# Attention with its scores computed a second time, keys on the partitions, and its keys and values projected in the first stage

## The reference

```python
x = x + einsum('bsd,sod->bso', layernorm(x), ctx_1024[itok])   # a weight matrix picked by position, 16 of them
x = x + moe_ffn(layernorm(x))            # 8 experts, top 1, exact gelu, times the gate
def xattn(query, key, value, mask, ...): # query = layernorm(x), key = value = ctx_1024
    q, k, v = (proj(t, W, b) for ...)    # 16 heads of 16
    scores = einsum('bhqd,bhkd->bhqk', q, k) / 4 + mask * -1e9   # mask [1, 1, 256, 256]
    ctx = einsum('bhqk,bhkd->bhqd', softmax(scores, axis=-1), v)
    return einsum('bsd,ed->bse', ctx, Wo) + bo
x = x + xattn(...)
x = x + nvfp4_linear(silu(nvfp4_linear(y, gate)) * nvfp4_linear(y, up), down)  # y = layernorm(x), 16-blocks, fp4 values, fp8 scales
```

## Time and profile before

| | |
|---|---|
| timed runs, us | 760.28 median of three (759.76, 760.28, 765.82) |
| profiled execution, us | 786.0, its span; mean granted clock 0.89 |
| busy in the span | TensorE 78%, VectorE 74%, ScalarE 51%, GpSimd 27% |
| first stage | 30 to 163 us |
| experts | 177 to 337 us |
| attention | 340 to 575 us |
| last stage | 576 to 786 us |

### The profile page before, as it was taken

How to read it: one execution, slowest core, us unless ns; L and a number is a source line. 1 busy time by engine, 2 the same in 40 slices (tenths; PEclk the granted TensorE clock), 3 DMA queues, 4 the chain that set the end, 5 groups by cost and what they waited for, 6 DMA issues and landing times.

```text
span 786.0 us, 14622 instructions
## 1 busy us (share of the span) xinstructions
PE 611.1 (78%) x4239; PEld 484.1 (62%) x4240; DVE 583.2 (74%) x1515; ACT 404.4 (51%) x780; POOL 209.1 (27%) x254
## 2 busy tenths in 40 slices
PE   5496786609899999958999999999744666766766
PEld 3384655409899898847888888887611433344424
DVE  6274666855645665667888889888648999999997
ACT  1341323003434233336565667665785798778762
POOL 5617363424644565510112222211100000000000
PEclk9698797858999999978999999999975799987998
DMA  8763242259375667261000000000000000000001
GB/s 321 228 209 118 71 137 76 96 181 385 107 232 173 185 197 230 78 185 34 1 0 0 0 0 0 0 1 1 2 3 1 0 27 27 13 27 13 27 27 54
DMA packets 35230, 68.22 MB, mean 87 GB/s; under 512 B 5405, under 2 KB 24238, under 8 KB 34160
## 3 DMA queue, kind: packets, MB, share of 16 engines
q1 hardware_dynamic: 28512, 52.20, 20.2%
q0 software_dynamic: 5520, 13.61, 5.1%
q10 hardware_dynamic: 1152, 1.88, 0.8%
HBM read 53.62 MB, written 15.80 MB: 88 GB/s over the span
## 4 chain that ended last, share of the span: by engine, by line
PE 36%; DVE 19%; issue 15%; ACT 13%; DMA 7%; another core or an unknown queue 3%; SPq 3%; POOL 2%; DVEq 1%; ACTq 0%; POOLq 0%
PE bank L1289 5%; PE quad L1162 4%; PE quad L1114 4%; PE quad L1273 3%; PE bank L1304 3%; PE bank L1171 3%; ACT hqT L1013 2%; DMA x_after_ffn<-row,niU 2%; PE quad L1454 2%; PE quad L1463 2%; ACT ctxs L996 2%; PE quad L1264 2%; DVE hh L2200 2%; DMA early<-in_W 2%
## 5 line engine op out<-in xcount | busy, mean ns | idle before, releaser
L746 ACT ACTIVATE hid<-quad,early 128x128 f32<-128x128 f32 x156 | 44.5, 368 | 87.8 <-PE quad L1162 86.5
L1162 PE MATMUL quad<-xts,early 128*128 128x128 f32 x624 | 76.5, 283 | 4.5 <-DMA early<-in_W 4.3
L1162 PEld LDWEIGHTS quad<-xts,early 128*128 128x128 f32 x624 | 74.9, 199 | 6.6 <-issue 5.5
L1171 PE MATMUL bank<-W2s,hid 128*128 x312 | 70.5, 379 | 0.0
L624 POOL TENSOR_TENSOR X<-fo,X 128x256 f32<-128x256 f32 (+1 forms) x32 | 21.8, 682 | 178.0 <-DVE fo L2046 178.0
L1289 PE MATMUL bank<-nVB,nPT 128*128 128x34 f32 x512 | 63.0, 279 | 0.0
L1171 PEld LDWEIGHTS bank<-W2s,hid 128*128 128x128 f32 x312 | 57.7, 190 | 7.1
L1289 PEld LDWEIGHTS bank<-nVB,nPT 128*128 128x128 f32 x512 | 59.6, 191 | 3.7
L1489 PE MATMUL bank<-dT,hqT 128*128 128x256 bf16 x224 | 41.0, 348 | 25.8 <-ACT hqT L1013 25.7
L577 POOL DMA_INDIRECT x_after_ffn<-row,niU x39 | 39.0, 1000 | 58.9 <-DVE row L1804 41.9
L1799 DVE SCALAR_TENSOR_TENSOR row<-bank,sco,row 128x256 f32<-128x256 f32 x39 | 18.5, 474 | 47.2 <-PE bank L1171 44.3
(11 more groups left out here) (325 smaller groups left out, 1431.6 us busy)
## 6 DMA issues: line engine op xcount, KB each, us to landing
early<-in_W SPq DMA_DIRECT2D x37, 514.0 KB
row<-rows_by_expert SPq DMA_DIRECT2D x38, 134.0 KB
early<-in_ctxO SPq DMA_DIRECT2D x4, 1024.0 KB, 7.8
ctxs<-in_ctxT SPq DMA_DIRECT2D x4, 1024.0 KB
W2s<-in_W SPq DMA_DIRECT2D x8, 512.0 KB
X<-x_after_ffn SPq DMA_DIRECT2D x7, 516.0 KB, 7.2
out<-yo SPq DMA_DIRECT2D x14, 256.0 KB, 2.1
early<-in_W ACTq DMA_DIRECT2D x2, 514.0 KB
```

The costliest lines, as they stand in the source:

```text
L746: ins = act.activation(hid[:, u, c * P:(c + 1) * P], bank[2 + u][:, c * P:(c + 1) * P], ACT.Gelu, bias=W1r[:, k, DC * H2 + c:DC * H2 + c + 1])
L1162: ins = pe.matmul(bank[2 + u][:, n * P:(n + 1) * P], W1r[:, m % RING, c * H2 + n * P:c * H2 + (n + 1) * P], xt[:, u, c, :], start=c == 0, ...
L1171: ins = pe.matmul(bank[6 + u % 2][:, 0:D], hid[:, u, c * P:(c + 1) * P], W2s[:, bass.ds(ex, 1), c, :].rearrange("p o s -> p (o s)"), start ...
```

## The change

The softmax of half a batch now takes two score products. The first (`score`, L1270) has queries on partitions as before, with the mask added by four bf16 matmuls (`onesb` x `maskb`, L1267), and serves the maxima alone: VectorE reduces them straight from PSUM (`row_max`). `maxima` splits the maxima of a batch in three bf16 parts, TensorE transposes them (`maxima_turn`), ScalarE evacuates (`maxima_out`). The second (`score_turned`) computes the scores with keys on partitions, [2 heads x 64 keys, 256 queries] eight times in two passes c, the maxima subtracted by a bf16 matmul with a selecting matrix (L1291). ScalarE takes the exponential straight from PSUM, the mask as its bias for each partition, and writes what `weigh` reads: the probabilities are no longer transposed, evacuated or shifted. `weigh` has the values (and for the sums a 0/1 matrix, `sumb`) as 32-column stationary tiles and 256 queries moving, and gives the values' elements on partitions, so that they need no transposing ahead of `project`. ScalarE inverts the sums (`inverse_sums`: Ln, then Exp of the negative), VectorE multiplies (`divide`), adds the projection to X in place (`add_rows`), and GpSimd has added the bias to X before (`biased`) and masks the keys (`keys_in`).

`keys_values` and `keys_values_out` stand in the first stage, one pair of batches in each of its groups 1 to 8. The loads of their weights stand ahead of the others. VectorE prepares the mask's parts at the end of the first stage. The flag gets a term: it fails where a key's mask differs between queries. The first tile's norm for the last stage now follows the last batch, where part of it stood inside the last batches. The flag's other terms, the experts and the last stage are as before.

The core of the diff, the new lines with their context; the lines that go stand in the listing above:

```diff
+Kall = sb("Kall", [P, NB // 2, DC, 2, KW], F32, ea)
+Vall = sb("Vall", [P, NB // 2, D], F32, ea)
...
+sp.dma_start(WkS[:], WkT).then_inc(s_kw, 16)
+sp.dma_start(WvS[:], WvT).then_inc(s_kw, 16)
+sp.dma_start(bkS[:], bk).then_inc(s_kw, 16)
...
+for t in range(2):
+  sp.dma_start(maskC[KW * t:KW * t + KW, :], maskT[S - KW:S, :]).then_inc(s_cw, 16)
+sp.dma_start(rowm[:, 0, :], mask[0, 0, S - KW:S].partition_broadcast(P)).then_inc(s_cw, 16)
...
+sp.wait_ge(s_dl, 1)
...
+  def keys_in(p, b, h, first=False):
+    if not first:
+      pool.wait_ge(n_ST, b * 2 - 2)
     pool.sem_inc(s_idle, 1)
+    pool.tensor_tensor(nKB[h][:].rearrange("p c (t s) -> p c t s", t=2),
+             Kall[:, bass.ds(p, 1), :, h, :].rearrange("p o c s -> p (o c) s").unsqueeze(2).broadcast_to([P, DC, 2, KW]),
+             own2[:].unsqueeze(1).unsqueeze(3).broadcast_to([P, DC, 2, KW]), ALU.mult).then_inc(n_kb, 1)
+  def biased(b):
+    pool.wait_ge(n_xn, b * 2 + 2)
+    pool.sem_inc(s_idle, 1)
+    xr = X2[:, bass.ds(b * 2 + 1, 2), 0:D]
+    pool.tensor_tensor(xr, xr, boS[:].unsqueeze(1).broadcast_to([P, 2, D]), ALU.add).then_inc(n_xb, 1)
+  def batch(b, h, p, k=None):
+    keys_in(p, b + 2, h)
+    biased(b + 2)
     if k is not None:
       weight_scaled(k)
...
+def keys_values_out(p):
+  act.wait_ge(s_kv, p + 1)
+  for n in range(DC):
+    act.activation(Kall[:, p, n], bank[6][:, n * P:(n + 1) * P].rearrange("p (b s) -> p b s", b=2),
+           ACT.Identity, bias=bkS[:, n:n + 1])
+  act.copy(Vall[:, p], bank[6][:, D:2 * D]).then_inc(s_kve, 1)
...
+  if 0 < g <= NB // 2:
+    keys_values_out(g - 1)
...
+  def maxima_out(b):
+    act.wait_ge(n_mT, b + 1)
+    act.copy(nMT[:], bank[0].bitcast(BF16)[:, 0:S]).then_inc(n_mTe, 1)
+  def exps(b, c):
+    act.wait_ge(n_ST, b * 2 + (c + 1))
+    act.activation(nPT[c][:], keyed, ACT.Exp, bias=keym[:, 0:1]).then_inc(n_exp, 1)
+  def values_in(p, b, h, first=False):
     if not first:
+      act.wait_ge(n_W, b * 2 - 2)
+    V4 = Vall[KW * h:KW * h + KW, bass.ds(p, 1), :].rearrange("s o (n t w) -> s (o n) t w", t=2, w=HD)
     for t in range(2):
+      ins = act.copy(nVB[h][KW * t:KW * t + KW, :, HD * t:HD * t + HD], V4[:, :, t, :])
     ins.then_inc(n_va, 1)
+  def inverse_sums(b, c):
+    act.wait_ge(n_W, b * 2 + (c + 1))
+    act.activation(nR[:, c, :], duo[:, c, S:2 * S], ACT.Ln).then_inc(n_ln, 1)
+    act.wait_ge(n_ln, b * 2 + (c + 1))
+    act.activation(nR[:, c, :], nR[:, c, :], ACT.Exp, scale=-1.0).then_inc(n_rv, 1)
+  def batch(b, h, p=None, first=False, k=None, stage=0):
+    exps(b, 0)
+    if stage < 2:
       queries_out(b + 1, 1 - h)
+    exps(b, 1)
+    if stage == 0:
+      rows_out(b + 2)
+    else:
+      weights_out(0 if stage == 1 else 3)
+    inverse_sums(b, 0)
+    if stage < 2:
+      values_in(p, b + 1, 1 - h, first)
+    if stage == 0 and b is not NB - 3:
+      rows_norm(b + 3)
+    if stage:
+      weights_out(1 if stage == 1 else 4)
+    inverse_sums(b, 1)
     if k is not None:
       weight_half(k, first=isinstance(k, int) and k == 0)
+    if stage < 2:
+      maxima_out(b + 1)
+    if stage:
+      weights_out(2 if stage == 1 else 5)
...
+  act.preload_act_table_set("natural_log_exp_and_others")
...
+def keys_values(p):
+  if p == 0:
+    pe.wait_ge(s_kw, 16 * 3)
+  pe.wait_ge(s_kve, p)
+  rows = [ctxs[:, 2 * p:2 * p + 2, c, S - KW:S] for c in range(DC)]
+  for n in range(DC):
+    for c in range(DC):
+      pe.matmul(bank[6][:, n * P:(n + 1) * P], WkS[:, c, n * P:(n + 1) * P], rows[c], start=c == 0, stop=c == DC - 1)
+  for h in range(2):
+    for c in range(DC):
+      ins = pe.matmul(bank[6][KW * h:KW * h + KW, D:2 * D], ctxs[:, 2 * p + h, c, S - KW:S],
+              WvS[:, c, :].rearrange("p (h w) -> p h w", w=VW)[:, :, 0:HD], start=c == 0, stop=c == DC - 1)
+  ins.then_inc(s_kv, 1)
...
+  def queries(bt, n):
+    if n == 0:
+      pe.wait_ge(n_xt, bt + 1)
     for c in range(DC):
+      ins = pe.matmul(bank[6][:, n * S:(n + 1) * S], WqS[:, c, n * P:(n + 1) * P], xt3[:, c, :],
+              start=c == 0, stop=c == DC - 1)
+    if n == DC - 1:
+      ins.then_inc(n_q, 1)
+  tiles = [slice(32 * k, 32 * k + 32) for k in range(4)]
   def score(b, h, q, first=False):
     if q == 0:
       pe.wait_ge(n_qe, b + 1)
       pe.wait_ge(n_kb, b + 1)
+      if not first:
+        pe.wait_ge(n_exp, b * 2)
     else:
+      pe.wait_ge(n_rd, b * 2 + 1)
+    for k, w in enumerate(tiles):
+      pe.matmul(scored[:, k, :], onesb[w, :], maskb[w, :], start=True, stop=False)
     for c in range(DC):
+      for k, w in enumerate(tiles):
         ins = pe.matmul(scored[:, k, c * P:(c + 1) * P], nQT[h][w, c, q * P:(q + 1) * P], nKB[h][w, c, :],
+                start=False, stop=c == DC - 1)
     ins.then_inc(n_S, 1)
+  def maxima_turn(b, first=False):
+    pe.wait_ge(n_mp, b + 1)
+    if not first:
+      pe.wait_ge(n_cn, b * 2)
+    for q in range(2):
+      ins = pe.transpose(bank[0].bitcast(BF16)[:, q * P:(q + 1) * P], nMb[:, q].rearrange("p k j -> p (k j)"), identb[:])
+    ins.then_inc(n_mT, 1)
+  def score_turned(b, h, c):
+    if c == 0:
+      pe.wait_ge(n_mTe, b + 1)
+      pe.wait_ge(n_rd, b * 2 + 2)
+    else:
+      pe.wait_ge(n_exp, b * 2 + 1)
+    for k, w in enumerate(tiles):
+      pe.matmul(keyed[:, k, :], selb[w, c * P:(c + 1) * P], nMT[w, :], start=True, stop=False)
+    for k, w in enumerate(tiles):
+      ins = pe.matmul(keyed[:, k, :], nKB[h][w, c, :], nQT[h][w, c, :], start=False, stop=True)
+    ins.then_inc(n_ST, 1)
+  def weigh(b, h, c, first=False):
+    pe.wait_ge(n_exp, b * 2 + (c + 1))
+    if c == 0:
+      pe.wait_ge(n_va, b + 1)
+    if not first:
+      pe.wait_ge(n_cn, b * 2 + (c - 1))
+    for k, w in enumerate(tiles):
+      pe.matmul(duo[w, c, 0:S], nVB[h][:, 4 * c + k, :], nPT[c][:, k, :], start=True, stop=True)
+    for k, w in enumerate(tiles):
+      ins = pe.matmul(duo[w, c, S:2 * S], sumb[:], nPT[c][:, k, :], start=True, stop=True)
+    ins.then_inc(n_W, 1)
+  def project(b, q, first=False):
     if q == 0:
+      pe.wait_ge(n_cn, b * 2 + 2)
     if first:
       pe.wait_ge(n_fo, 1)
     else:
+      pe.wait_ge(n_ad, b * 2 + q)
     for k in range(DC):
+      ins = pe.matmul(bank[7][:, 0:D], nC[:, k, q * P:(q + 1) * P], WoS[:, k, :], start=k == 0, stop=k == DC - 1)
     ins.then_inc(n_wo, 1)
+  def batch(b, h, first=False, stage=0):
+    score_turned(b, h, 0)
     if not first:
       project(b - 1, 1)
+    score_turned(b, h, 1)
+    weigh(b, h, 0, first)
+    if stage == 0:
+      rows_in(b + 2)
+    if stage == 1:
+      pe.wait_ge(n_qe, NB)
+    if stage:
+      weights_in(0 if stage == 1 else 3)
+    if stage < 2:
       score(b + 1, 1 - h, 0)
+    weigh(b, h, 1, first)
+    if stage == 0:
+      queries(b + 2, 0)
+    else:
+      weights_in(1 if stage == 1 else 4)
+    if stage < 2:
+      score(b + 1, 1 - h, 1)
+    if stage == 0:
+      queries(b + 2, 1)
+    else:
+      weights_in(2 if stage == 1 else 5)
+    project(b, 0, first)
+    if stage < 2:
+      maxima_turn(b + 1)
...
+st.put(red(bound[:, 6:7], mrow[:, 2, :], AX.X, ALU.max))
+def key_mask():
+  red(keym[:, 0:1], maskC, AX.X, ALU.max)
+  st.link(red(keym[:, 1:2], maskC, AX.X, ALU.min))
+  st.link(tt(keym[:, 1:2], keym[:, 0:1], keym[:, 1:2], ALU.subtract))
+  st.link(ts(keym[:, 1:2], keym[:, 1:2], 0.0, 1.0e30, ALU.is_gt, ALU.mult))
+  tt(bound[:, 6:7], bound[:, 6:7], keym[:, 1:2], ALU.add)
...
+  def row_max(b, q):
     v.wait_ge(n_S, b * 2 + (q + 1))
+    red(nM[:, q, :].rearrange("p (k m) -> p k m", k=4), scored.rearrange("p k (m s) -> p k m s", m=4),
+      AX.X, ALU.max).then_inc(n_rd, 1)
+  def maxima(b):
+    v.wait_ge(n_rd, b * 2 + 2)
+    m, r = (a[:].rearrange("p q (k j) -> p q k j", k=4) for a in (nM, nMr))
+    parts = [nMb[:, :, :, 4 * n:4 * n + 4] for n in range(3)]
+    stn.link(v.tensor_copy(parts[0], m))
+    stn.link(tt(r, m, parts[0], ALU.subtract))
+    stn.link(v.tensor_copy(parts[1], r))
+    tt(parts[2], r, parts[1], ALU.subtract).then_inc(n_mp, 1)
+  def divide(b, c):
+    v.wait_ge(n_rv, b * 2 + (c + 1))
+    tt(nC[:, c, :], duo[:, c, 0:S], nR[:, c, :], ALU.mult).then_inc(n_cn, 1)
+  def add_rows(b, q):
+    if q == 0:
+      v.wait_ge(n_xb, b + 1)
     v.wait_ge(n_wo, b * 2 + (q + 1))
+    v.sem_inc(s_idle, 1)
+    xr = X2[:, bass.ds(b * 2 + (q + 1), 1), 0:D].rearrange("p o d -> p (o d)")
+    tt(xr, bank[7][:, 0:D], xr, ALU.add).then_inc(n_ad, 1)
   def new_stats(b, q):
+    v.wait_ge(n_ad, b * 2 + (q + 1))
     return v.bn_stats(st2[:, bass.ds(b * 2 + (q + 1), 1), :].rearrange("p o w -> p (o w)"),
              X2[:, bass.ds(b * 2 + (q + 1), 1), 0:D].rearrange("p o d -> p (o d)"))
   inverse_rows(0, stn)
   v.wait_ge(n_bo, 1)
   tt(boS[:], boS[:], bank[7][:, 0:D], ALU.add).then_inc(n_fo, 1)
+  inverse_rows(1, stn)
+  row_max(0, 0)
   weight_scales(stn)
+  row_max(0, 1)
+  v.wait_ge(n_z, 1)
+  maxima(0)
   weight_rounding(stn)
   weight_inverses(stn, 0)
+  def batch(b, first=False, between=None):
+    if not first:
+      add_rows(b - 1, 1)
+      new_stats(b - 1, 1)
```

(19 more changed lines are left out.)

437 lines of the change are left out of this document (128 added, 309 removed).

## The result

| | before | changed |
|---|---|---|
| timed runs, us | 762.82 (756.06 to 768.5, 20) | 767.32 (762.0 to 772.78, 20) |
| ratio to before, 95% interval | | 1.0066 (1.0042 to 1.0089) |
| profiled execution, span us | 756.1 (a second one, below) | 761.7 |
| last scatter of the first stage ends | 139.94 | 145.41 |
| flag computed | 310.66 | 318.58 |

The forecast was 750 with a range of 737 to 772: the time lies in the range, but it moved 4.5 us up where 10 down were forecast. The changed kernel is slower by 0.66%, which is little and nevertheless clear of noise. The column "before" uses a second profiled execution of the same kernel, run as one of the experiments: its landmarks compare stage by stage.

What follows compares the result with a forecast made beforehand. TensorE bounds the old attention at 12.75 us a batch; in the new loop a circle of waits sets 10.96. Terms -20.1 + 9.3 + 0.4 = -10.4 took the profiled 786.0 to 775.6, the median 760.3 to 750; range 737 to 772.

Steps and rivals of the forecast that it cites:

- The circle of waits: Attention loop: waits through three engines, from one batch's first turned scores to the next's, set the period at 10.96 us.
- tiles one by one: Rival, weighing in the attention loop: column tiles do not run at once, 15.6 us a batch, kernel 820; chance 0.03.
- failed flag: Rival: the flag with its new term fails and general attention over 256 keys runs, over 1000 us; chance 0.03.
- The clock: Rival, attention loop: TensorE's waiting lowers its clock; low level 30% of the time gives 12.6 a batch, kernel 774; chance 0.12.
- Keys early: First stage: projecting keys and values there makes TensorE bound eight groups, some 10.95 us each; +9.3 us.
- stand-still: First stage, profiled execution: stretches with nearly all engines standing, 25.5 us, taken as hardly present in the timed runs.
- Into and out of the loop: Attention's start and tail: laid out with 15 periods, the gate starts at 555.1 against 575.20, -20.1 us for attention.
- cold start: Ahead of the loop's first turned score: some 3 us more for the pipe's start, after 359.7.
- The mask's parts: End of the first stage: some 25 small VectorE operations, 5 us, where it waits 7.04 us for rows; +0.4.

Runs made afterwards that it cites:

- GpSimd later: Changed kernel with GpSimd's weight scaling waiting until VectorE has written the maxima's parts: 752.26 us, ratio 0.9876 to the kernel before.
- keys late: Changed kernel with all eight pairs of keys and values projected behind the first stage's last ranks, four evacuations ahead of ScalarE's zero-filling transfers: 767.85 us, ratio 1.0077 to before.

## Why the prediction was wrong, step by step

**The circle of waits was right.** In the batch from 361.30 its hops stand, from the first turned score: second turned scores 1.97 (forecast 1.92), weighing 2.63 (2.60), rows out 4.32 (4.26), Ln 4.81 (4.77), Exp 5.23 (5.20), values 5.67 (5.52), norms 6.30 (5.94), second Ln 7.29 (6.92), divide 8.13 (7.81), row maximum 8.47 (8.15), maxima 9.72 (9.29), next batch 11.46 (10.96). Most of the 0.5 is in the values (they start 0.44 behind the Exp, not 0.32, and take 0.63, not 0.42) and in the reduction, which holds VectorE 1.25, not 1.14. The prediction's own prices were 0.42 for the Exp and 0.52 for the values; its circle laid both 0.1 shorter. These rows show it:

```profile
365.62 0.58 ACT L851 COPY xt<-bank 128x512 f32<-128x512 f32 x1 [0.44 <-PE bank L1243]
366.11 0.39 ACT L878 ACTIVATE nR<-duo 128x256 f32<-128x256 f32 x1
366.53 0.42 ACT L880 ACTIVATE nR<-nR 128x256 f32<-128x256 f32 x1
366.97 0.60 ACT L873 COPY nVB<-Vall 64x128 f32<-64x128 f32 x2
367.60 1.09 ACT L846 ACTIVATE xn<-X,nm,rs 128x256 f32<-128x256 f32 x2
368.59 0.36 ACT L878 ACTIVATE nR<-duo 128x256 f32<-128x256 f32 x1
368.99 0.42 ACT L880 ACTIVATE nR<-nR 128x256 f32<-128x256 f32 x1
```

Ln and Exp cost 0.39 and 0.42 where 0.43 and 0.42 were taken. Column tiles ran at once: the eight weighings span 1.0 us, as taken. The rival with tiles one by one and the one of a failed flag are out.

**The step that failed** is the sentence "GpSimd's two or three operations (0.7 each) have ten us of cover. The weights' preparations hide: without them the circle is unchanged." Cover in time was there; what was not asked is what runs on VectorE meanwhile. The maxima stand on the circle, in the very gap in which GpSimd got its weights. Five batches without weights took 57.1 us for forecast 54.8; the eight with them 104.7 for 87.7; the last two 22.9 for 22.2: 184.7 where 164.7 were forecast. Of the 20, 6.6 are the circle's 0.46 a batch over its forecast, in all fifteen, and 13.4 are the weights': seven gaps of TensorE are longer than 0.88, by 5.8 together, and six pairs of exponentials are further apart than 1.97, by 6.9 together. That term the prediction put at nothing. The Trainium skill says this ("SBUF — State Buffer", Who interferes with whom): a VectorE instruction with two SBUF inputs, or a copy or cast in a two-port mode, contends with GpSimd for a port pair that is locked for a whole instruction, and a reduction does not. The trace agrees: the cast 0.18 to 0.56, the subtraction 0.19 to 0.65, each ending 0.04 behind a GpSimd product, the reduction from PSUM 1.21 to 1.23 throughout. No run here shows which mode the cast runs in.

**The clock was a rival and came in part**, with the wrong condition. It was priced as a share of the time that grows with TensorE's waiting over a whole batch; the batch with TensorE busy for 9.85 of 11.46 us kept 2.4 GHz throughout. It fell where most of the waiting lay in one piece of 1.7 us, and cost up to 1.3 of the period, since only the projection and the second turned scores stood in the slow stretch. Its price was near: the granted clock over the loop (338.50 to 523.20) was 0.94, a low level for 12% of the time, which by the prediction's own sum is an estimated 9 us, and 6.9 were measured. That the time fell inside the range is owed to the high end that this rival set, not to the forecast.

**Keys early**: +9.3 forecast, +5.5 measured. The groups are 10.75 apart where 10.95 were laid out, and the stage without keys ends at 139.94, not at the 137.3 of my layout. 2.6 of the error was in the base and 1.2 in the groups, and the 25.5 us read as stand-still were 22.9 (162.80 less 139.94).

**Into and out of the loop**: 22.8 us were forecast from the flag (339.93 in the first profile) to the first turned score, 19.9 measured (the 3 us of cold start did not appear here; in the other profiled runs the first batch is up to 2.5 us longer than this one's 11.52, in the run with GpSimd later with a granted clock of 0.55 from 338 to 344); from the last batch's start to the last transposed weights 11.2 forecast, 9.5 measured; from the last transposed weights to the first gate product 16.4 forecast, 16.4 measured (532.65 to 549.06).

**The mask's parts were mis-sized.** They were put at +0.4, since VectorE waited 7.04 us for the experts' first rows. That wait belongs to the slow first profile; in the second one it is 2.10 (first row, the kernel before). In the changed kernel the rows' loads start at 149.04, 6.0 later than before, but VectorE is busy without a break until 155.5, from 150.8 on with these parts, and its first norm starts 8.4 later:

```profile
147.13 1.38 DVE L1755 TENSOR_SCALAR xn<-row 128x256 f32<-128x256 f32 x4 [2.10 <-DMA row<-rows_by_expert]
```

```profile
155.31 0.19 DVE L1779 MEMSET sumb<- 64x16 f32 x2
155.52 1.38 DVE L1797 TENSOR_SCALAR xn<-row 128x256 f32<-128x256 f32 x4
```

With keys late VectorE had finished the parts and waited for the rows again:

```profile
155.32 1.38 DVE L1801 TENSOR_SCALAR xn<-row 128x256 f32<-128x256 f32 x4 [4.79 <-DMA row<-rows_by_expert]
```

There the norm starts 3.5 behind the loads at 151.79, before 4.1 behind them, and in the changed kernel 6.5. Of the 8.4 us, 5.5 are the scatters', 0.5 the loads' later start behind them and 2.4 VectorE's, and at the flag 7.9 are left: the experts' 2.4 us are in the main these. No run tested it by moving the parts elsewhere.

Taken together, from the forecast of -10.4: +20.0 in the loop, -2.9 and -1.7 around it, -3.8 for the keys, +2.0 for the mask's parts, +0.7 since the kernel before takes 234.55 from flag to first gate product in its second profile and 235.27 in its first, and +1.7 in the last stage: 5.6. The last stage is open: it takes 210.8 and 210.9 in the two profiles of the kernel before and 212.3 to 216.5 in those of the changed kernel and of all its variants, so it is longer in each, in most by more than in the changed kernel itself, and nothing that the change touches there was found.

## What to carry to other kernels

Before calling an engine's work hidden, look at what the other engines do at that moment, not only at whether it has time: here GpSimd's products made small VectorE operations on the path three times as long. Put such work where VectorE reduces from PSUM or is idle; here a wait for that was worth 15 us. Read TensorE's idle time by its pieces: a gap 0.84 us longer cost up to 1.3 more in clock, where idle time in pieces of up to 0.9 cost no clock in most batches. And a wait read from a slow execution is no cover: VectorE's 7.04 us were 2.10 in a usual one.
